# A transformer layer on eight cores: the output projection of two heads spread over the two heads behind them, with more buffers and the transposes in another PSUM pair

## Chip, cores and metric

The kernel runs on one Trainium2 chip, on all 8 cores. Each core works on one sequence of 2048 tokens, with no exchange between cores. The metric is the device time in microseconds of the slowest core; a change of under 2% counts as none.

## What is computed

One layer with pre-normalisation, per sequence of shape 2048 x 1024, 8 heads of 256, a latent of 64 for keys and values, and a gated feed-forward part of width 3072 with integer weights:

```python
q = (x @ Wq.T).reshape(b, t, N_HEADS, HEAD_DIM)
kv_latent = x @ Wkv_down.T                    # 64 wide
k = (kv_latent @ Wk_up.T).reshape(...)
v = (kv_latent @ Wv_up.T).reshape(...)
attn = softmax(einsum('bqhd,bkhd->bhqk', q, k) * HEAD_DIM ** (-0.5))
out = einsum('bhqk,bkhd->bqhd', attn, v)
x = x + out.reshape(b, t, -1) @ Wo.T          # all on layernorm(x)
h = silu(xn @ wg.T) * (xn @ wu.T)             # xn = layernorm(x), w = int / 127
x = x + h @ wd.T
```

## The kernel before

**Work of a head.** The kernel never forms k, v or the full q. As the latent has only 64 values, it folds Wk_up into Wq and Wv_up into Wo for each head, and attention runs in the latent space. All activations are held with features on partitions. Names used below, with the lines of the kernel before:

- `emit_prepA`, `emit_prepB` (L283, L303): the folded query weight, 64 x 1024, and its transpose, which goes into the buffer WAT. PE writes both into PSUM pair PD, VectorE copies them out (L299, L321).
- `emit_prepC` (L326): the folded output weight of the head, 64 x 1024, into one of the MSB buffers (L342).
- `emit_Qp(h, tb)` (L347): the latent query of 512 tokens, 8 matmuls of 128 rows into a bank of PB.
- `emit_Spair(h, j, kp)` (L411): the scores of query block j (512 tokens, j from 0 to 3) against two blocks of 128 keys: two matmuls of 64 rows into PA or PD in turn; ScalarE takes the exponential of both (L434).
- `emit_PVg(h, j, qs)` (L442): 16 matmuls of 65 columns for 128 queries, the last column being the sum of the exponentials, into bank qs % 2 of PC. VectorE evacuates it with three instructions: a copy of the sum (L452), a reciprocal (L454), a product (L457) into the buffer UTM.
- `emit_UT(h, oct)` (L461): 8 small matmuls that transpose 1024 tokens of that result; ScalarE copies them into a buffer UFM (L486).
- `emit_WO2(h1, o, oct)` (L491), called a unit here: the output projection of two heads, h1 - 1 and h1, for 128 features o and 1024 tokens. It is 4 matmuls of 64 rows, 2 for each bank of PB or PC (in turn from unit to unit), and one add of VectorE onto x (L507). A pair of heads has 16 units.

**PSUM.** There are four pairs of banks, PA to PD, 1024 columns of float32 each. `bank_free` holds for each bank the instruction that last emptied it, and `pe_group` makes the first matmul of a group wait for it. A unit has two groups, one for each bank, so it has two such waits.

**Order.** Every engine works in the order in which the builder emits. Waits are on counters of the engines. The order is written by hand: the loop of a head (L657) first has block 0 of the scores, then for j = 1, 2, 3 and i = 0 to 3, called slot (j, i), two score pairs of block j, a PV group of block j - 1, and then what `fill` holds for the slot. For the next head these are prepA in (1,1), prepB in (2,1), Qp in (2,3), (3,0), (3,2), (3,3), and prepC in (3,1). The even heads 2, 4 and 6 have in addition the 16 units of the pair before them, two in each of the slots (1,0) to (2,3), ahead of what else stands there. Heads 0, 1, 3, 5 and 7 have none. Behind the slots come the four PV groups of block 3, the first score pairs of the next head and the two transposes. At the end of an odd head, four more score pairs, (nxt, 1, 0) to (nxt, 1, 3), are computed ahead, so that slots (1,0) and (1,1) of heads 2, 4 and 6 have none left. Behind head 7 come its transposes and the 16 units of heads 6 and 7, then the second layer norm and the feed-forward part.

**Buffers.** `arena` is one tensor in SBUF with offsets set by hand. MSB has three buffers of 1024 columns, used by h % 3; UFM is one area of two buffers, used by h % 2.

Of the kernel before, what the change touches and what calls it, by code (L numbers as in the profile page):

```python
# [18 lines left out]
NCH = 8  # L19
# [24 lines left out]
QP = QH  # L44
KVT = KH
WAB = KH + 1040
WAT = (VH, VH + 512)
MSB = (VH + 1024, VH + 2048, VH + 3072)
UTM = ZT
UFM = ZF  # L50
HHB = RA
WDB = VH
WG = (WQ0, WQ0 + 1024)
# [57 lines left out]
def build_program(tap=None):  # L111
# [22 lines left out]
    ar = ar_t.ap()  # L134
# [7 lines left out]
    PA = nc.alloc_psum_tensor("PA", [128, 1024], F32).ap()  # L142
    PB = nc.alloc_psum_tensor("PB", [128, 1024], F32).ap()
# [115 lines left out]
    qpev = [[None] * NTB for _ in range(H)]  # L259
    prepA_ev = [None] * H  # L260
    wat_done = [None, None]
    msb_done = [None] * 3
    ut_done = [[None, None], [None, None]]
    q_mm_done = [0] * H
    wo_mm_done = [0] * H
    wo_add_last = [0] * NCH
# [59 lines left out]
    def emit_prepC(h):  # L326
        key = ("prepC", h)
        if key in emitted:
            return
        emitted.add(key)  # L330
        wob = wo_base[h % 2]
        g = None
        for half in (0, 1):
            g = pe_group(
                PD[0:64, half * 512:(half + 1) * 512], [("PD", half)],
                [(ar[:, WVU + (h * 2 + c) * 64: WVU + (h * 2 + c + 1) * 64],
                  ar[:, wob + c * 1024 + half * 512:
                     wob + c * 1024 + (half + 1) * 512])
                 for c in (0, 1)],
                waits=[(sWS, ws_all), (sWO[h % 2], 16 * (h // 2 + 1))])  # L340
# [120 lines left out]
    def emit_UT(h, oct_):  # L461
        key = ("UT", h, oct_)
        if key in emitted:
            return
        emitted.add(key)
        ti = s_rot[0] % 2
        s_rot[0] += 1
        P = (PA, PD)[ti]
        keys = [("PA", 0), ("PA", 1)] if ti == 0 else [("PD", 0), ("PD", 1)]
        w = [(sDVE, zev_done[(h, 2 * oct_ + 1, 3)]), (sPOOL, pool_init)]  # L470
        for k in keys:
            tf = bank_free.get(k)
            if tf:
                w.append(tf)
        for i in range(8):
            tc = oct_ * 8 + i
            b.emit("tensor", lambda e, tc=tc, i=i, P=P: e.matmul(
                P[0:64, i * 128:(i + 1) * 128],
                ar[:, UTM + tc * 64: UTM + (tc + 1) * 64],
                ident, start=True, stop=True),  # L480
                waits=w if i == 0 else (),
                inc=sPE if i == 7 else None)
        g = sPE.n
        ub = UFM + (h % 2) * 2048
        dst = ar[0:64, ub + oct_ * 1024: ub + (oct_ + 1) * 1024]
        v = consume("scalar", lambda e, P=P, d=dst: e.activation(  # L486
            d, P[0:64, 0:1024], AF.Copy),
            keys, waits=[(sPE, g)], inc=sACT)
        ut_done[h % 2][oct_] = (sACT, v)

    def emit_WO2(h1, o, oct_):  # L491
        P, pk = ((PB, "PB"), (PC, "PC"))[wo_pair[0] % 2]
        wo_pair[0] += 1
        h0 = h1 - 1
        g = None
        for n in (0, 1):
            tb = oct_ * 2 + n
            g = pe_group(
                bank(P, n), [(pk, n)],
                [(ar[0:64, MSB[hh % 3] + o * 128: MSB[hh % 3] + (o + 1) * 128],  # L500
                  ar[0:64, UFM + (hh % 2) * 2048 + tb * 512:
                     UFM + (hh % 2) * 2048 + (tb + 1) * 512])
                 for hh in (h0, h1)],
                waits=[msb_done[h0 % 3], msb_done[h1 % 3],
                       ut_done[0][oct_], ut_done[1][oct_]])
        wo_add_last[o] = consume(
            "vector", lambda e, P=P, o=o, oc=oct_: e.tensor_add(  # L507
                x[:, o * T + oc * 1024: o * T + (oc + 1) * 1024], P[:, 0:1024],
                x[:, o * T + oc * 1024: o * T + (oc + 1) * 1024]),
            [(pk, 0), (pk, 1)], waits=[(sPE, g), (sX, 16)], inc=sDVE)  # L510
# [146 lines left out]
    for h in range(H):  # L657
# [15 lines left out]
        if nxt < H:  # L673
# [289 lines left out]
```

How the kernel before makes its waits and increments, by code:

```python
        def run(e, wl=wl, fn=fn, after=after):  # L100
            for (hh, v) in wl:
                e.wait_ge(hh, v)
            inst = fn(e)
            if after is not None:
                inst.then_inc(after[0], after[1])
# [5 lines left out]
def build_program(tap=None):  # L111
# [764 lines left out]
                b.emit("sync", lambda e, o=o: e.dma_start(  # L876
                    out=out_d[o * 128:(o + 1) * 128, :],
                    in_=x[:, o * T:(o + 1) * T]),
                    waits=[(sDVE, down_add_final)], inc=sST)
        down_b1_done[0] = sPE.n
        if half == 0:
            for c in range(NHALF, NFC):
                load_wd(c, [(sPE, down_b1_done[0])] if c == NHALF else [])
    fin = sST.n
    b.emit("sync", lambda e: e.wait_ge(sST.h, fin))
    with nc.Block() as block:
        @block.tensor
```

## Time and profile before

| | us |
|---|---|
| median of 2 runs | 1258.91 (1257.81 and 1260.01) |
| the profiled execution | 1260.86 |
| its span on core 4, the slowest (the cores: 1249.8 to 1259.0) | 1259.0 |
| PE busy with matmuls | 1116.6 (89%) |
| VectorE busy | 358.0 (28%) |
| ScalarE busy | 417.1 (33%) |
| GpSimd busy | 55.1 (4%) |

The span is the time from the first to the last instruction of a core. All rows and times below are of core 4, in us from the start of its span. The profile's page has a line with the clock that TensorE was granted in each fortieth of the span, in tenths of 2.4 GHz. There are two levels, 1.2 GHz (0.50) and 2.4 GHz (1.00); numbers in between are means over a stretch. Attention fills the time up to about 695 us, the rest is the second layer norm and the feed-forward part.

### The profile page before, as it was taken

The numbers are of one execution on the slowest core, as the hardware profiler recorded it, in microseconds if no ns is written. First come the engines' busy times: TensorE is split into PE (matmuls) and PEld (weight loads), VectorE is DVE, ScalarE is ACT, GpSimd is POOL, SyncE is SP. The second block draws the span as 40 slices with busy tenths as digits, with TensorE's granted clock in tenths as the row PEclk, the third lists the DMA queues.
The fourth block names the chain that finished last, engine by engine and source line by source line (L and its number), as shares of the span: only waits on it lengthen the run. The fifth ranks groups of instructions, "written<-read, shape, count | busy, mean of one in ns | idle before, by whom it ended". The sixth has DMA issues, their size and how long they took to land.

```text
span 1259.0 us, 15601 instructions; the slowest of 8 cores (1249.8 to 1259.0 us)
## 1 busy us (share of the span) xinstructions
PE 1116.6 (89%) x5873; PEld 477.0 (38%) x5921; DVE 358.0 (28%) x674; ACT 417.1 (33%) x402; POOL 55.1 (4%) x110
## 2 busy tenths in 40 slices
PE   7656989898898998889899577999999999999998
PEld 3112433333343343433343122444444444444443
DVE  0573222243223441334226452010112201010122
ACT  0313565523644346532674122233200022233000
POOL 2000000000000000000001200000000020000000
PEclk9876576756666575855856677999999999999999
DMA  8941101010110010000005902222210082221122
GB/s 131 250 124 17 18 17 18 17 18 7 28 18 1 17 18 1 1 1 1 1 1 101 163 4 33 35 34 42 42 17 1 1 135 34 42 42 18 67 101 100
DMA packets 17561, 54.08 MB, mean 43 GB/s; under 512 B 1744, under 2 KB 1872, under 8 KB 15440
## 3 DMA queue, kind: packets, MB, share of 16 engines
q0 software_dynamic: 15296, 36.31, 18.1%
q1 hardware_dynamic: 2192, 16.78, 3.6%
q8 instruction: 48, 0.79, 0.3%
q14 instruction: 25, 0.20, 0.1%
HBM read 72.61 MB, written 8.39 MB: 64 GB/s over the span
## 4 chain that ended last, share of the span: by engine, by line
PE 76%; ACT 10%; DVE 7%; DMA 3%; issue 3%; DVEq 0%; ACTq 0%; POOL 0%; POOLq 0%
PE PB L179 23%; PE PA L179 19%; PE PC L179 18%; PE PD L179 15%; ACT arena L434 7%; DMA arena<-x 2%; DVE arena L624 1%; DVE arena L622 1%; DVE x_fm L507 1%; ACT arena L486 1%; DVE arena L342 1%; DVE arena L299 1%; ACT arena L527 1%; DVE arena L321 0%; DMA arena<-x_fm 0%
## 5 line engine op out<-in xcount | busy, mean ns | idle before, releaser
L179 PE MATMUL PA<-arena 128*128 128x512 bf16 (+2 forms) x1066 | 301.4, 424 | 30.6 <-DMA arena<-x 9.2
L179 PE MATMUL PB<-arena 128*128 128x512 bf16 (+2 forms) x1129 | 305.7, 422 | 3.3 <-DVE arena L321 1.3
L179 PE MATMUL PC<-arena 128*128 128x65 bf16 (+3 forms) x2584 | 277.9, 272 | 23.2 <-DVE arena L624 16.6
L179 PE MATMUL PD<-arena 128*128 128x512 bf16 (+3 forms) x774 | 249.0, 452 | 39.6 <-ACT arena L434 22.7
L179 PEld LDWEIGHTS PC<-arena 128*128 128x128 bf16 (+2 forms) x2592 | 158.6, 117 | 196.0 <-issue 151.1
L434 ACT ACTIVATE arena<-PA 128x1024 bf16<-128x1024 f32 x121 | 123.8, 1023 | 272.8 <-PE PA L179 258.2
L179 PEld LDWEIGHTS PB<-arena 128*128 128x128 bf16 (+2 forms) x1152 | 118.9, 108 | 152.1 <-issue 43.3
L179 PEld LDWEIGHTS PA<-arena 128*128 128x128 bf16 (+2 forms) x1074 | 99.1, 101 | 180.7 <-issue 84.6
L434 ACT ACTIVATE arena<-PD 128x1024 bf16<-128x1024 f32 x135 | 138.1, 1023 | 28.7 <-PE PD L179 18.0
L179 PEld LDWEIGHTS PD<-arena 128*128 128x128 bf16 (+3 forms) x782 | 77.1, 106 | 177.1 <-issue 120.3
L826 DVE TENSOR_TENSOR arena<-arena 128x1024 bf16<-128x1024 bf16 x48 | 33.2, 692 | 302.1 <-ACT arena L817 302.1
L452 DVE COPY t<-PC 128x1 f32<-128x1 f32 x128 | 20.2, 158 | 243.1 <-PE PC L179 241.1
L812 ACT ACTIVATE arena<-PA 128x1024 bf16<-128x1024 f32 x24 | 24.6, 1023 | 137.6 <-PE PA L179 137.6
L507 DVE TENSOR_TENSOR x_fm<-PB,x_fm 128x1024 f32<-128x1024 f32 x32 | 39.2, 1224 | 29.2 <-PE PB L179 29.1
L812 ACT ACTIVATE arena<-PC 128x1024 bf16<-128x1024 f32 x24 | 24.6, 1023 | 57.5 <-PE PC L179 57.4
L507 DVE TENSOR_TENSOR x_fm<-PC,x_fm 128x1024 f32<-128x1024 f32 x32 | 39.2, 1225 | 15.0 <-PE PC L179 13.9
L817 ACT ACTIVATE arena<-PD 128x1024 bf16<-128x1024 f32 x24 | 24.6, 1023 | 56.7 <-PE PD L179 56.7
L817 ACT ACTIVATE arena<-PB 128x1024 bf16<-128x1024 f32 x24 | 24.6, 1023 | 54.6 <-PE PB L179 54.6
L457 DVE TENSOR_SCALAR arena<-PC,rc 128x64 bf16<-128x64 f32 x128 | 36.3, 284 | 13.7
L871 DVE TENSOR_TENSOR x_fm<-PB,x_fm 128x1024 f32<-128x1024 f32 x16 | 19.6, 1224 | 63.3 <-PE PB L179 63.3
L871 DVE TENSOR_TENSOR x_fm<-PA,x_fm 128x1024 f32<-128x1024 f32 x16 | 19.6, 1224 | 62.0 <-PE PA L179 62.0
L362 DVE CAST arena<-PB 64x512 bf16<-64x512 f32 x32 | 21.8, 683 | 49.1 <-PE PB L179 49.1
(71 smaller groups left out, 311.9 us busy)
## 6 DMA issues: line engine op xcount, KB each, us to landing
x_fm<-x SPq DMA_DIRECT2D x1, 8192.0 KB, 43.1
out<-x_fm SPq DMA_DIRECT2D x8, 1024.0 KB, 3.8
arena<-wg POOLq DMA_DIRECT2D x24, 256.0 KB, 3.9
arena<-wu POOLq DMA_DIRECT2D x24, 256.0 KB, 3.6
arena<-wd POOLq DMA_DIRECT2D x24, 256.0 KB, 15.0
arena<-x POOLq DMA_DIRECT2D x1, 4096.0 KB, 30.4
arena<-wq POOLq DMA_DIRECT2D x8, 512.0 KB, 5.7
arena<-wo POOLq DMA_DIRECT2D x8, 512.0 KB, 5.5
```

Source lines behind the costliest of these rows:

```text
L179: e.matmul(o, l, r, start=st, stop=sp)),
L299: prepA_ev[h] = consume("vector", lambda e: e.tensor_copy(ar[0:64, WAB:WAB + 1024], PD[0:64, 0:1024]), [("PD", 0), ("PD", 1)], waits=[(sPE ...
L342: v = consume("vector", lambda e, h=h: e.tensor_copy(ar[0:64, MSB[h % 3]:MSB[h % 3] + 1024], PD[0:64, 0:1024]), [("PD", 0), ("PD", 1)], wa ...
L362: v = consume("vector", lambda e, a=qa, d=dst: e.tensor_copy(d, a[0:64, :]), [qk], waits=[(sPE, g)], inc=sDVE)
L434: "scalar", lambda e, P=P, p=pbuf, kp=kp: e.activation(ar[:, p + kp * 1024: p + (kp + 1) * 1024], P[:, 0:1024], AF.Exp, scale=SC_ATTN),
L452: b.emit("vector", lambda e, a=za: e.tensor_copy(t1[:, 0:1], a[:, 64:65]), waits=[(sPE, g)], inc=sDVE)
L457: "vector", lambda e, a=za, tc=tc: e.tensor_scalar_mul(ar[:, UTM + tc * 64: UTM + (tc + 1) * 64], a[:, 0:64], rc),
L507: "vector", lambda e, P=P, o=o, oc=oct_: e.tensor_add(x[:, o * T + oc * 1024: o * T + (oc + 1) * 1024], P[:, 0:1024], x[:, o * T + oc * 10 ...
L812: "scalar", lambda e, t=t: e.activation(ar[:, SCR_S:SCR_S + 1024], G_ap[t][:, 0:1024], AF.Silu, scale=INV127),
L817: "scalar", lambda e, t=t: e.activation(ar[:, SCR_U:SCR_U + 1024], U_ap[t][:, 0:1024], AF.Copy, scale=INV127 * INV127),
L826: "vector", lambda e, hcol=hcol: e.tensor_mul(ar[:, hcol:hcol + 1024], ar[:, SCR_S:SCR_S + 1024], ar[:, SCR_U:SCR_U + 1024]),
L871: "vector", lambda e, P=P, o=o, tp=tp: e.tensor_add(x[:, o * T + tp * 1024: o * T + (tp + 1) * 1024], P[:, 0:1024], x[:, o * T + tp * 1024 ...
```

## The change

It has three parts.

1. Units of a pair of heads are spread over two heads. The first eight (o from 0 to 3) stay in the even head behind the pair, the other eight (o from 4 to 7) move to the odd head after it. Each of the slots (1,0) to (2,3) of heads 2 to 7 now has one unit. The 16 units behind head 7 stay.
2. For that, buffers must live longer: MSB has four buffers (h % 4), UFM three (h % 3). WAT moves to free columns in the key area, and MSB takes the place that it had.
3. The transposes of `emit_UT` go to PB, both of them. Before, they took PA or PD in turn with the score pairs.

```diff
-WAT = (VH, VH + 512)
-MSB = (VH + 1024, VH + 2048, VH + 3072)
+WAT = (KH + 2064, KH + 2576)
+MSB = (VH, VH + 1024, VH + 2048, VH + 3072)
 UTM = ZT
-UFM = ZF
+UFM = (ZF, ZF + 2048, ZT + 1024)
...
-    msb_done = [None] * 3
-    ut_done = [[None, None], [None, None]]
+    msb_done = [None] * 4
+    ut_done = [[None, None] for _ in range(3)]
...
     def emit_UT(h, oct_):
...
-        ti = s_rot[0] % 2
-        s_rot[0] += 1
-        P = (PA, PD)[ti]
-        keys = [("PA", 0), ("PA", 1)] if ti == 0 else [("PD", 0), ("PD", 1)]
+        P = PB
+        keys = [("PB", 0), ("PB", 1)]
...
-        ub = UFM + (h % 2) * 2048
+        ub = UFM[h % 3]
...
     def emit_WO2(h1, o, oct_):
...
-                waits=[msb_done[h0 % 3], msb_done[h1 % 3],
-                       ut_done[0][oct_], ut_done[1][oct_]])
+                waits=[msb_done[h0 % 4], msb_done[h1 % 4],
+                       ut_done[h0 % 3][oct_], ut_done[h1 % 3][oct_]])
...
+        wu = []
         if h % 2 == 0 and h > 0:
-            wu = [(o, oc) for o in range(NCH) for oc in (0, 1)]
-            for idx, (o, oc) in enumerate(wu):
-                slot = (1 + idx // 8, (idx % 8) // 2)
-                fill.setdefault(slot, []).insert(0, (lambda o=o, oc=oc:
-                                                     emit_WO2(h - 1, o, oc)))
+            wu = [(h - 1, o, oc) for o in range(4) for oc in (0, 1)]
+        elif h % 2 == 1 and h >= 3:
+            wu = [(h - 2, o, oc) for o in range(4, NCH) for oc in (0, 1)]
+        for idx, (h1, o, oc) in enumerate(wu):
+            slot = (1 + idx // 4, idx % 4)
+            fill.setdefault(slot, []).insert(0, (lambda h1=h1, o=o, oc=oc:
+                                                 emit_WO2(h1, o, oc)))
```

How PE's order moves, at three places. All rows are PE's, in the order of the program, with the counter that a matmul waits for, if any (sACT is ScalarE's, sDVE VectorE's). 128x65 is a PV group, 128x512 into PA or PD a score pair, 128x512 into PB or PC a unit, 64x512 into PD prepA, 64x128 a transpose.

Head 2, slots (1,0) and (1,1) with prepA behind them, before:

```order
L179 MATMUL PC<-arena 128x65 x16
L179 MATMUL PB<-arena 128x512 x4
L179 MATMUL PC<-arena 128x512 [waits sDVE]
L179 MATMUL PC<-arena 128x512 x3
L179 MATMUL PC<-arena 128x65 [waits sDVE]
L179 MATMUL PC<-arena 128x65 x15
L179 MATMUL PB<-arena 128x512 x4
L179 MATMUL PC<-arena 128x512 x2
L179 MATMUL PC<-arena 128x512 [waits sDVE]
L179 MATMUL PC<-arena 128x512
L179 MATMUL PD<-arena 64x512 [waits sWQ1,sACT]
```

The same place after the change:

```order
L179 MATMUL PC<-arena 128x65 x16
L179 MATMUL PB<-arena 128x512 x4
L179 MATMUL PC<-arena 128x65 x16
L179 MATMUL PC<-arena 128x512 [waits sDVE]
L179 MATMUL PC<-arena 128x512
L179 MATMUL PC<-arena 128x512 [waits sDVE]
L179 MATMUL PC<-arena 128x512
L179 MATMUL PD<-arena 64x512 [waits sWQ1,sACT]
```

The second PV group no longer waits for VectorE, and the unit in PC stands directly behind it, with a wait ahead of each half.

Head 3, slot (1,1) with prepA behind it, before:

```order
L179 MATMUL PA<-arena 128x512 [waits sACT]
L179 MATMUL PA<-arena 128x512
L179 MATMUL PD<-arena 128x512 [waits sACT]
L179 MATMUL PD<-arena 128x512
L179 MATMUL PC<-arena 128x65 x16
L179 MATMUL PD<-arena 64x512 [waits sWQ0,sACT]
```

The same place after the change:

```order
L179 MATMUL PA<-arena 128x512 [waits sACT]
L179 MATMUL PA<-arena 128x512
L179 MATMUL PD<-arena 128x512 [waits sACT]
L179 MATMUL PD<-arena 128x512
L179 MATMUL PC<-arena 128x65 x16
L179 MATMUL PC<-arena 128x512 [waits sDVE]
L179 MATMUL PC<-arena 128x512
L179 MATMUL PC<-arena 128x512 [waits sDVE]
L179 MATMUL PC<-arena 128x512
L179 MATMUL PD<-arena 64x512 [waits sWQ0,sACT]
```

A unit in PC stands between the PV group and prepA. Slots with an even i have their unit in PB.

Behind head 7, the transposes and the first units, before:

```order
L477 MATMUL PA<-arena 64x128 x8
L477 MATMUL PD<-arena 64x128 [waits sDVE]
L477 MATMUL PD<-arena 64x128 x7
L179 MATMUL PB<-arena 128x512 [waits sACT]
L179 MATMUL PB<-arena 128x512 x3
```

The same place after the change:

```order
L475 MATMUL PB<-arena 64x128 x8
L475 MATMUL PB<-arena 64x128 [waits sDVE,sACT]
L475 MATMUL PB<-arena 64x128 x7
L179 MATMUL PB<-arena 128x512 [waits sACT]
L179 MATMUL PB<-arena 128x512 x3
```

The second transpose waits for ScalarE too, and both it and the first unit use the pair that the first transpose used.

## Rows read from the trace of the kernel before

**Rows 1.** The page: granted TensorE clock in 40 slices, in tenths.

```profile
PEclk9876576756666575855856677999999999999999
```

**Rows 2.** Stretches of heads 3 and 6: busy us of each engine, then the clock.

```profile
324.20:384.60 60.40, 53.93 (x385) 23.40 (x386) 15.77 (x56) 34.85 (x35) 1.06 (x2) 0.66 0.10 18
531.10:619.50 88.40, 79.65 (x449) 32.00 (x450) 35.11 (x71) 34.80 (x35) 0.00 (x0) 0.63 0.00 1
```

**Rows 3.** Stretches within heads 1 and 2, columns PE, PEld, DVE, ACT, POOL, clock, DMA.

```profile
211.10:221.30 10.20, 7.89 (x60) 3.44 (x58) 3.79 (x9) 4.87 (x5) 0.53 (x1) 1.00 0.00 0
...
262.00:283.00 21.00, 21.00 (x91) 8.33 (x90) 10.27 (x19) 6.14 (x6) 0.00 (x0) 0.50 0.04 7
...
298.00:306.70 8.70, 8.70 (x35) 3.63 (x35) 2.51 (x5) 2.05 (x2) 0.00 (x0) 0.50 0.01 3
306.70:327.20 20.50, 16.78 (x174) 8.37 (x171) 7.50 (x25) 12.01 (x12) 0.53 (x1) 1.00 0.16 27
```

**Rows 4.** Order of time, PE, head 3: start, us, instruction, idle before and releaser.

```profile
337.66 1.89 PE L179 MATMUL PD<-arena 128*64 128x512 bf16 x4 [0.58 <-ACT arena L434]
...
345.83 1.03 PE L179 MATMUL PA<-arena 64*128 64x512 bf16 x2
...
348.64 1.03 PE L179 MATMUL PA<-arena 64*128 64x512 bf16 x2
...
352.11 0.58 PE L314 MATMUL PD<-arena 64*128 64x64 bf16 x8 [0.59 <-ACT arena L434]
...
353.70 1.01 PE L179 MATMUL PD<-arena 64*128 64x512 bf16 x2 [0.16 <-DVE arena L321]
```

**Rows 5.** Order of time, PE, head 2, slots (1,0) and (1,1).

```profile
245.35 1.06 PE L179 MATMUL PC<-arena 128*128 128x65 bf16 x16
246.34 1.88 PE L179 MATMUL PB<-arena 64*128 64x512 bf16 x4
248.02 1.91 PE L179 MATMUL PC<-arena 64*128 64x512 bf16 x4
251.48 1.04 PE L179 MATMUL PC<-arena 128*128 128x65 bf16 x16 [1.55 <-DVE x_fm L507]
```

**Rows 6.** Order of time, VectorE, the same place.

```profile
246.58 0.16 DVE L452 COPY t<-PC 128x1 f32<-128x1 f32 x1 [12.14 <-PE PC L179]
...
247.11 0.28 DVE L457 TENSOR_SCALAR arena<-PC,rc 128x64 bf16<-128x64 f32 x1
248.47 1.22 DVE L507 TENSOR_TENSOR x_fm<-PB,x_fm 128x1024 f32<-128x1024 f32 x1 [1.07 <-PE PB L179]
```

**Rows 7.** Order of time, PE, single places in heads 1, 2 and 7.

```profile
209.92 2.49 PE L179 MATMUL PB<-arena 128*64 128x512 bf16 x8
...
236.41 0.61 PE L477 MATMUL PA<-arena 128*64 128x128 bf16 x8 [0.52 <-ACT arena L486]
...
286.33 1.01 PE L179 MATMUL PD<-arena 64*128 64x512 bf16 x2 [1.06 <-DVE arena L321]
...
298.01 3.62 PE L179 MATMUL PB<-arena 128*64 128x512 bf16 x8
...
661.05 1.92 PE L179 MATMUL PC<-arena 128*128 128x65 bf16 x32 [0.70 <-DVE rc L454]
663.23 1.96 PE L179 MATMUL PC<-arena 128*128 128x65 bf16 x32 [0.26 <-DVE arena L457]
```

**Rows 8.** Order of time, ScalarE and PE, the transposes and first units behind head 7.

```profile
665.90 1.02 ACT L486 ACTIVATE arena<-PA 64x1024 bf16<-64x1024 f32 x1 [5.11 <-PE PA L477]
666.32 0.61 PE L477 MATMUL PD<-arena 128*64 128x128 bf16 x8 [0.57 <-DVE arena L457]
667.06 1.02 PE L179 MATMUL PB<-arena 64*128 64x512 bf16 x4
667.08 1.02 ACT L486 ACTIVATE arena<-PD 64x1024 bf16<-64x1024 f32 x1 [0.16 <-PE PD L477]
668.24 1.02 PE L179 MATMUL PC<-arena 64*128 64x512 bf16 x4 [0.16 <-ACT arena L486]
```

More of the change, by code:

```diff
@@ L342, in emit_prepC @@
         v = consume("vector", lambda e, h=h: e.tensor_copy(
-            ar[0:64, MSB[h % 3]:MSB[h % 3] + 1024], PD[0:64, 0:1024]),
+            ar[0:64, MSB[h % 4]:MSB[h % 4] + 1024], PD[0:64, 0:1024]),
             [("PD", 0), ("PD", 1)], waits=[(sPE, g)], inc=sDVE)
-        msb_done[h % 3] = (sDVE, v)
+        msb_done[h % 4] = (sDVE, v)
     def emit_Qp(h, tb, eng="vector"):
@@ L488, in emit_UT @@
             keys, waits=[(sPE, g)], inc=sACT)
-        ut_done[h % 2][oct_] = (sACT, v)
+        ut_done[h % 3][oct_] = (sACT, v)
     def emit_WO2(h1, o, oct_):
@@ L499, in emit_WO2 @@
                 bank(P, n), [(pk, n)],
-                [(ar[0:64, MSB[hh % 3] + o * 128: MSB[hh % 3] + (o + 1) * 128],
-                  ar[0:64, UFM + (hh % 2) * 2048 + tb * 512:
-                     UFM + (hh % 2) * 2048 + (tb + 1) * 512])
+                [(ar[0:64, MSB[hh % 4] + o * 128: MSB[hh % 4] + (o + 1) * 128],
+                  ar[0:64, UFM[hh % 3] + tb * 512:
+                     UFM[hh % 3] + (tb + 1) * 512])
                  for hh in (h0, h1)],
-                waits=[msb_done[h0 % 3], msb_done[h1 % 3],
-                       ut_done[0][oct_], ut_done[1][oct_]])
+                waits=[msb_done[h0 % 4], msb_done[h1 % 4],
+                       ut_done[h0 % 3][oct_], ut_done[h1 % 3][oct_]])
         wo_add_last[o] = consume(
@@ L740, in build_program @@
             maybe_tap("u0", ar[:, UTM:UTM + 1024], [(sDVE, zev_done[(0, 3, 3)])])
-            maybe_tap("uf0", ar[0:64, UFM:UFM + 2048], [ut_done[0][1]])
+            maybe_tap("uf0", ar[0:64, UFM[0]:UFM[0] + 2048], [ut_done[0][1]])
     pe_attn_done = sPE.n
```

## Prediction

> **What bounds the kernel now.** I read the page first, then stretches by head, then the order of time on TensorE (PE). The page's line of the granted clock has 5 to 8 tenths in slices 2 to 25 of 40, which hold all of attention, and 9 after them [rows 1]. The stretches by head say the same: head 3, which today has no output-projection units, takes 60.4 us at a mean clock of 0.66; head 6, which has sixteen, 88.4 us at 0.63; ScalarE is busy some 34.8 us in either, so it is not what bounds a whole head [rows 2]. Each head has two phases. In its slots (1,0) to (2,3) the clock stands at 1.2 GHz (0.50); from the query projection Qp of the next head to the head's end it is mostly at 2.4 GHz [rows 3]. All units of emit_WO2, before and after the change, lie in the slow phase of their heads, apart from the sixteen behind head 7.
>
> In that phase PE has no slack. In head 3 one slot (two score pairs and a PV group) goes from 345.83 to 348.64, 2.81 us [rows 4]. A unit costs PE 248.02 - 246.34 = 1.68 us on top [rows 5]. From 262 to 283 us, where each slot of head 2 has two units, PE is busy 21.00 of 21.00 us at 0.50 [rows 3].
>
> **Eight units moved per pair of heads.** Eight units leave heads 2, 4 and 6 (8 x 1.68 = 13.4 us each) and eight enter heads 3, 5 and 7 (13.4 us each). No work is removed, both places run on a PE-bound stretch at the same clock, so the sum is nil: 3 x (13.4 - 13.4) = 0. ScalarE gains nothing either: a slot with one unit is 2.81 + 1.68 = 4.5 us of PE against two exponentials, each of about the 1.02 us that ScalarE's copies of the same width take [rows 8]. What is left is waits.
>
> A page of the Trainium skill speaks for more. "TensorE: Matmul & The Clock Gate", Part 1, says that the clock goes by how busy PE has been and that sustained activity brings full rate. By that, filling the idle time of the light heads would lift them to 2.4 GHz. The trace disagrees: the stretch from 262 to 283 us is full and stays at 0.50 [rows 3]. By the rule the sum would be that of rival C; by the rows it is nil.
>
> **Waits that go.** (a) Slot (1,1) of heads 2, 4 and 6 has its score pairs computed ahead, so the PV group stands directly behind a unit in PC and waits 1.55 us for VectorE's add [rows 5]. After the change one unit in PB stands ahead of it, and that wait goes: -1.55 x 3. (b) In heads 3 and 5 prepA waits 0.58 us and prepB 0.59 us for the exponential in PD [rows 4]. The PC unit now ahead of each hides that: -1.17 x 2.
>
> **Waits that come.** (c) With one unit per slot, PB and PC take turns by slot, so slots with odd i have PV in bank 1 of PC and, directly behind it, the unit in PC. Its second half needs bank 1, which is free when VectorE has evacuated the PV group. In head 2 a PV group starts at 245.35 [rows 5]; its evacuation starts with the copy at 246.58 and ends at 247.11 + 0.28 = 247.39 [rows 6], 2.04 us after the start of PV. With 0.14 us from an end to the next start (668.10 to 668.24 [rows 8]) the bank is free at 2.18. PE gets there after the PV group (246.34 - 245.35 = 0.99 us) and half a unit (0.84), at 1.83. So it waits 0.35 us. Today the PB unit in between covers this. There are four such slots in each of six heads, 24, less the three of (d): 21 x 0.35 = +7.4. Queued behind the waiting matmul are the rest of the unit and, in order, everything else of PE; nothing else can fill the time.
> (d) In slot (1,1) of heads 2, 4, 6 VectorE first adds the PB unit: from 248.47 for 1.22 us, to 249.69 [rows 6]. PV starts at 248.02 already, its evacuation (0.81 us from the copy's start to its end) only after 249.69, so it ends at 250.50 and the bank is free at 250.64. PE arrives at 248.02 + 0.99 + 0.84 = 249.85: +0.79 x 3.
> (e) prepB in heads 3 and 5: the second score pair behind it waits for the copy of L321, 0.16 us today [rows 4]. With a unit's add ahead of that copy on VectorE it will wait as in head 2, 1.06 us [rows 7]: +0.90 x 2.
> (f) The transposes of head 7: both now use PB. The second starts at 666.32 today [rows 8]; it must then wait for ScalarE's copy of the first (665.90 + 1.02 + 0.14 = 667.06), +0.74. Its own copy starts 0.76 us after it (667.08 - 666.32), takes 1.02, and the first output unit, in PB too, starts 0.14 later: 667.06 + 0.76 + 1.02 + 0.14 = 668.98 against 667.06 today: +1.92. The units behind it go at the pace of VectorE or PE as before.
> (g) In heads 0 to 6 the transposes lose nothing: the second waits for ScalarE's copy of the first today too (0.52 us at 236.41 [rows 7]), through PA. The score pairs between them no longer share a bank with them, but ScalarE is then working back to back. I count nil, at best 0.2 us per head.
> The moved buffers cost nothing: no instruction is added, and no load waits for them before the end of attention. A wait on a third buffer of transposed values or a fourth of MSB comes a head later than its last reader.
>
> Sum: -4.65 - 2.34 + 7.35 + 2.37 + 1.80 + 1.92 = +6.5 us. The only term without a direct row is (c). Other waits of PE for the evacuation of a PV group are 0.70 and 0.26 us [rows 7]; below, it cannot be under 0, since a bank is either free or waited for. With 0 the sum is -0.9, with 0.70 it is +13.8. I take 0.35, which is worked out of starts and ends of the same three instructions and lies next to the 0.26. The profiled execution took 1260.86 us (span 1259.0); 1260.86 + 6.5 = 1267.4. The median of the plain runs, 1258.91, is 1.95 us below the profiled one, so I predict 1265.4 us, 0.5% over it.
>
> **Rivals.** A is the forecast.
> B: the waits of (c) are hidden, PE reaching bank 1 when it is free. For it: the margin is a third of a microsecond, and PE idles elsewhere in some slots. Against: (c) comes from unhurried rows. 1258.9 - 0.9 = 1258.0 us.
> C: light heads filled with units come up to 2.4 GHz. A slot of 4.5 us would take half, 2.25 (ScalarE's two exponentials just fit): 2.25 x 8 slots x 3 heads = 54 us, 1265.4 - 54 = 1211 us. Against: both a stretch with no units (light slots) and one with two per slot stay at 0.50, and one unit per slot lies between them. Only the rule of the Trainium skill quoted above speaks for it.
> D: the clock comes up later in heads 3 and 5. In head 1, without units, it is up from 211.1; Qp(nxt,0) had begun at 209.92. In head 2, with units just ahead of Qp, it comes up only at 306.7, and Qp had begun at 298.01: 0.50 from 298 to 306.7 [rows 3, 7]. If the unit ahead of Qp does this, heads 3 and 5 lose up to 8 us each of full clock, worth up to half, some 3.5 us each: 1265.4 + 7 = 1272.4.
> E, the other side: D in its strong form. The unit and its wait directly ahead of Qp keep the clock at 1.2 GHz for the whole 20.5 us that head 2 now has at 2.4 GHz [rows 3]. PE is busy 16.78 us of these [rows 3], which is up to 33.6 at half rate, 13 us more than the stretch takes now. Two heads of it already decide (25 us is 2%): 1265.4 + 26 = 1291. Against: the sixteen-unit heads have two units directly ahead of Qp and come up all the same.
>
> **How the numbers follow.** A 0.53, B 0.15, C 0.04, D 0.24, E 0.04. A's own range is 1261 to 1270; the cores of this run differ by 9 us in when their clock falls and rises, and each head can shift by a few. B adds 1258 below, D 1274 above: 1257 to 1274, with C and E left out. A change of under 2% is about what a measurement of this kernel cannot tell from none; faster by over 2% is C (0.04), slower by over 2% is E (0.04), the rest 0.92.
>
> **What would show it.** In the new trace: PC matmuls waiting for the last step of a PV evacuation 24 times, 0.35 us each and 0.8 in three; the 1.55 us waits for the add gone; heads 2 to 6 all 72 to 77 us; the light heads' slots at 0.50 and 4.5 us; the first unit behind head 7 some 1.9 us after the second transpose, 0.7 today. If slots of head 3 run at 2.4 GHz, or the waits of (c) are absent, or Qp(nxt,0) of head 3 begins over 5 us before the clock comes up, the forecast is wrong at that step.

## The result, and the profile after

| | median us | ratio to the kernel before, 95% interval |
|---|---|---|
| kernel before, beside it | 1260.31 | |
| changed kernel | 1265.86 | 1.0052 [1.0038, 1.0065] |

The change costs half a per cent, 5.6 us; 0.5% was forecast, 6.5 us, and 1265.4 us. That 1265.4 and 1265.86 lie so close is in part luck: the forecast started from 1258.91 us for the kernel before, which measures 1260.31 here, and its difference was 1 us too large.

The slowest core is now core 6, and the rows after the change are of that core. Its span went from 1258.9 us to 1264.5; averaged over the eight cores the span went from 1255.1 to 1262.4 us, since the cores lay further apart before. The page's line of the granted clock answers to [rows 1]:

```profile
PEclk9777586758576575857655777999999999999999
```

It still has 5 to 8 tenths all through attention. The six heads that now hold eight units each, as stretches with the busy time of PE, PEld, VectorE, ScalarE and GpSimd, then the clock; they answer to [rows 2]:

```profile
231.80:306.30 74.50, 65.84 (x417) 26.12 (x416) 25.31 (x63) 34.73 (x35) 1.06 (x2) 0.66 0.09 15
306.30:381.40 75.10, 67.55 (x418) 27.10 (x417) 25.38 (x64) 34.60 (x35) 1.06 (x2) 0.64 0.09 15
381.40:457.80 76.40, 67.58 (x417) 26.80 (x416) 25.32 (x64) 34.97 (x35) 1.06 (x2) 0.64 0.09 14
457.80:533.00 75.20, 67.71 (x418) 27.23 (x417) 25.34 (x64) 34.78 (x35) 0.00 (x0) 0.64 0.00 1
533.00:607.10 74.10, 66.06 (x418) 26.20 (x417) 25.34 (x64) 34.77 (x35) 0.00 (x0) 0.65 0.00 1
607.10:668.30 61.20, 55.93 (x362) 24.64 (x361) 19.16 (x55) 31.79 (x32) 0.00 (x0) 0.53 0.00 1
```

Heads 2 to 6 now have one length, 74.1 to 76.4 us, where they had 58 to 60 and 88 to 90 in turn. That is what the spreading does: it moved time and saved none.

The new waits stand in PE's order of time, in head 2: start, duration, instruction, idle before it and its releaser. They answer to [rows 5].

```profile
244.22 1.89 PE L179 MATMUL PB<-arena 64*128 64x512 bf16 x4
246.04 2.03 PE L179 MATMUL PC<-arena 128*128 128x65 bf16 x18
248.64 1.01 PE L179 MATMUL PC<-arena 64*128 64x512 bf16 x2 [0.57 <-DVE arena L457]
...
258.49 2.03 PE L179 MATMUL PC<-arena 128*128 128x65 bf16 x18
260.69 1.01 PE L179 MATMUL PC<-arena 64*128 64x512 bf16 x2 [0.17 <-DVE arena L457]
```

"x18" is the PV group (16) with the first half of the unit (2), since both write PC. In the second case, slot (1,3), it starts at 258.49, and the second half follows at 260.69: 2.20 us, where the prediction had 2.18. Without a wait PE would have been there after 1.83, so the wait costs 0.37 us. The bracket says only 0.17, as the end of a matmul is modelled in the profile and here lies some 0.2 us behind the point at which the next may start. Whoever adds up brackets would count half of this wait. In slot (1,1) of head 2 it is 248.64 - 246.04 = 2.60, so 0.77 us (0.79 forecast).

The waits of PE in total, from 160 to 700 us (engine, line, releaser: us in total, times, longest):

```profile
PE PB L475 <- ACT arena L484: 10.8, 8, 1.5
...
PE PC L179 <- DVE arena L457: 5.8, 25, 0.6
PE PD L179 <- DVE arena L321: 5.5, 6, 1.1
...
PE PB L179 <- ACT arena L484: 1.3, 1, 1.3
```

25 waits for L457: the 24 forecast and the one that was already there at the end of head 7 [rows 7]. None for the add of a unit is left; that was the 1.55 us wait of [rows 5]. The place behind head 7, which answers to [rows 8]:

```profile
668.27 1.06 PE L475 MATMUL PB<-arena 128*64 128x128 bf16 x8
...
670.65 0.61 PE L475 MATMUL PB<-arena 128*64 128x128 bf16 x8 [1.31 <-ACT arena L484]
...
672.57 1.74 PE L179 MATMUL PB<-arena 64*128 64x512 bf16 x4 [1.31 <-ACT arena L484]
```

From the second transpose to the first unit it is 1.92 us, as forecast.

Where did the 5.6 us of this core come from? The starts of the first transpose of each head, read from the order of time of core 6, give the account. I name an interval by the head whose slots it holds, and give before, after and what is left when the 13.4 us of moved units are taken out:

| interval | before | after | left | forecast |
|---|---|---|---|---|
| up to the first transpose of head 0 | 173.83 | 173.63 | -0.2 | 0 |
| head 1 | 60.12 | 58.16 | -2.0 | 0 |
| head 2 | 90.08 | 74.55 | -2.1 | +0.3 |
| head 3 | 60.34 | 75.05 | +1.3 | +1.1 |
| head 4 | 88.11 | 76.42 | +1.7 | +0.3 |
| head 5 | 58.40 | 75.19 | +3.4 | +1.1 |
| head 6 | 88.38 | 74.10 | -0.9 | +0.3 |
| head 7 | 45.64 | 61.17 | +2.1 | +1.4 |
| from the transposes of head 7 to the end | 594.0 | 596.2 | +2.2 | +1.9 |

Heads 2 to 7 have +5.5 together and +4.5 was forecast. On core 0 they have 436.5 us against 428.9, +7.5. Single heads are off by up to 2.4 us to either side. Head 1 is off by 2.0 us, though its slots are unchanged: its mean granted clock on core 6 was 0.66 before and is 0.71 now, while core 0 has 0.71 and 58.15 us in both kernels. So part of the differences of single heads is the clock, to which the experiments come.

### The profile page after: what moved, and what is told of

Same layout as the page of the kernel before. It is cut to its first block, busy times and chain, and to the rows that moved or that the text cites. A ratio compares the mean times of both kernels' runs of the same rounds, so it can differ in the third digit from the quotient of the medians.

```text
span 1264.5 us, 15636 instructions; the slowest of 8 cores (1260.0 to 1264.5 us)
## 1 busy us (share of the span) xinstructions
PE 1120.6 (89%) x5921; PEld 471.6 (37%) x5921; DVE 358.1 (28%) x674; ACT 417.0 (33%) x402; POOL 55.1 (4%) x110
## 4 chain that ended last, share of the span: by engine, by line
PE 74%; ACT 9%; DVE 9%; issue 3%; DMA 3%; DVEq 0%; ACTq 0%; POOL 0%; POOLq 0%
PE PB L179 24%; PE PA L179 19%; PE PC L179 17%; PE PD L179 15%; ACT arena L434 6%; DMA arena<-x 3%; ACT arena L484 1%; DVE arena L620 1%; DVE arena L622 1%; DVE x_fm L505 1%; DVE arena L299 1%; DVE arena L342 1%; ACT arena L525 1%; DVE arena L457 1%; DVE arena L321 0%
## 5 line engine op out<-in xcount | busy, mean ns | idle before, releaser
L179 PE MATMUL PA<-arena 128*128 128x512 bf16 (+2 forms) x1088 | 306.6, 423 | 24.1 <-DMA arena<-x 10.2
L179 PE MATMUL PC<-arena 128*128 128x65 bf16 (+3 forms) x2592 | 281.1, 272 | 23.1 <-DVE arena L622 16.6
L179 PE MATMUL PD<-arena 128*128 128x512 bf16 (+3 forms) x768 | 242.6, 449 | 42.2 <-ACT arena L434 24.8
L179 PEld LDWEIGHTS PC<-arena 128*128 128x128 bf16 (+2 forms) x2592 | 150.1, 115 | 193.6 <-issue 147.3
L434 ACT ACTIVATE arena<-PA 128x1024 bf16<-128x1024 f32 x128 | 130.9, 1023 | 273.3 <-PE PA L179 260.3
L179 PEld LDWEIGHTS PA<-arena 128*128 128x128 bf16 (+2 forms) x1088 | 103.0, 102 | 184.8 <-issue 89.3
L434 ACT ACTIVATE arena<-PD 128x1024 bf16<-128x1024 f32 x128 | 131.0, 1023 | 29.8 <-PE PD L179 20.9
L813 ACT ACTIVATE arena<-PA 128x1024 bf16<-128x1024 f32 x24 | 24.6, 1023 | 137.6 <-PE PA L179 137.6
L818 ACT ACTIVATE arena<-PD 128x1024 bf16<-128x1024 f32 x24 | 24.6, 1023 | 55.6 <-PE PD L179 55.6
L457 DVE TENSOR_SCALAR arena<-PC,rc 128x64 bf16<-128x64 f32 x128 | 36.3, 284 | 14.2 <-DVE rc L454 0.8
```

The lines of the kernel that those rows point to most:

```text
L179: e.matmul(o, l, r, start=st, stop=sp)),
L434: "scalar", lambda e, P=P, p=pbuf, kp=kp: e.activation(ar[:, p + kp * 1024: p + (kp + 1) * 1024], P[:, 0:1024], AF.Exp, scale=SC_ATTN),
L457: "vector", lambda e, a=za, tc=tc: e.tensor_scalar_mul(ar[:, UTM + tc * 64: UTM + (tc + 1) * 64], a[:, 0:64], rc),
L813: "scalar", lambda e, t=t: e.activation(ar[:, SCR_S:SCR_S + 1024], G_ap[t][:, 0:1024], AF.Silu, scale=INV127),
L818: "scalar", lambda e, t=t: e.activation(ar[:, SCR_U:SCR_U + 1024], U_ap[t][:, 0:1024], AF.Copy, scale=INV127 * INV127),
```

## The experiments

Each ran beside the kernel before on the same chip; the ratio is always to that kernel.

**1. Units in PB.** The waits for bank 1 of PC are taken away by giving the units of the slots to PB, except in slot (2,3), where Qp follows in PB.

```diff
-    def emit_WO2(h1, o, oct_):
-        P, pk = ((PB, "PB"), (PC, "PC"))[wo_pair[0] % 2]
-        wo_pair[0] += 1
+    def emit_WO2(h1, o, oct_, pair=None):
+        if pair is None:
+            pair = wo_pair[0] % 2
+            wo_pair[0] += 1
+        P, pk = ((PB, "PB"), (PC, "PC"))[pair]
...
-            fill.setdefault(slot, []).insert(0, (lambda h1=h1, o=o, oc=oc:
-                                                 emit_WO2(h1, o, oc)))
+            fill.setdefault(slot, []).insert(0, (lambda h1=h1, o=o, oc=oc, pair=int(idx == 7):
+                                                 emit_WO2(h1, o, oc, pair)))
```

> The changed kernel, with the units of the slots in PB, all but the one of slot (2,3), which stays in PC. Theory (the waits for bank 1 of PC cost what they take, 0.37 us from start to start): they go in 15 places (three slots each in six heads, less slot (1,1) of heads 2, 4 and 6, where the unit now waits about as long, 0.8 us, for the add of the unit ahead in PB), 15 x 0.37 = 5.5 us. The ratio to the kernel before falls from 1.005 to about 1.001. In the trace PE waits for L457 six or seven times outside head 7's end instead of 25. Rival (the time of the new kernel goes by when the clock comes up, and a few tenths of a microsecond of waits disappear in it): within 1.5 us of the changed kernel, ratio 1.004 to 1.006, although the waits are gone.

Measured: 0.9996 [0.9982, 1.0009]. Against the changed kernel's 1.0052 that is 0.56%, or 7 us; 5.5 were expected. The waits in the trace (core 0), 160 to 700 us:

```profile
PE PB L179 <- DVE x_fm L507: 1.7, 3, 0.6
...
PE PC L179 <- DVE arena L457: 1.3, 7, 0.3
```

Seven waits for L457 instead of 25, and three for the add, in slot (1,1) of heads 2, 4 and 6, as expected. So the units in PC are what makes the changed kernel slower: with them in PB the whole slowdown is gone. The waits themselves are 5.5 us of it. Heads 2 to 7 are 8.7 to 14.1 us shorter than in the changed kernel, core by core, so the edit also changed something beside the waits; run 5 comes back to it.

**2. Transposes back in PA and PD.**

```diff
-        P = PB
-        keys = [("PB", 0), ("PB", 1)]
+        ti = s_rot[0] % 2
+        s_rot[0] += 1
+        P = (PA, PD)[ti]
+        keys = [("PA", 0), ("PA", 1)] if ti == 0 else [("PD", 0), ("PD", 1)]
```

> The changed kernel, with the transposes back in PA and PD in turn with the score pairs. Theory (the new place of the transposes costs only behind head 7, where the second waits for the copy of the first, and the first unit for the copy of the second): 2.4 us less than the changed kernel, ratio 1.003; from the first transpose of head 7 to the first unit about 1.9 us instead of 4.3. Rival (it costs nothing, since the units behind it catch up, or it gains in the other heads): no change from 1.005, or above.

Measured: 1.0038 [1.0022, 1.0054], 0.14% or 1.8 us below the changed kernel. The difference is no larger than the two intervals allow, so the time alone shows little. The rows behind head 7 (core 4) do:

```profile
666.63 1.06 PE L477 MATMUL PA<-arena 128*64 128x128 bf16 x8
667.84 0.61 PE L477 MATMUL PD<-arena 128*64 128x128 bf16 x8
669.00 1.02 PE L179 MATMUL PB<-arena 64*128 64x512 bf16 x4 [0.56 <-ACT arena L486]
```

2.37 us from the first transpose to the first unit instead of 4.30: 1.93, where the forecast for this term was 1.92. The expected 1.9 us for this stretch was off, since the clock had not yet come up there (the first transpose takes 1.06 us, against some 0.6 at 2.4 GHz; in the kernel before the clock comes up with it).

**3. Both edits.** The spreading and its buffers are left, with seven of a head's eight units in PB.

> Both edits: units of the slots in PB but for slot (2,3), and the transposes in PA and PD as before. Only the spreading of the units is left of the change. Theory: the two savings add up, 5.5 + 2.4 = 7.9 us below the changed kernel, ratio about 0.999, which says that the spreading alone is neutral. Rival (spreading alone costs, by later rises of the clock in heads 3 to 5): ratio 1.002 or more.

Measured: 0.9962 [0.9945, 0.9979]. It is faster than the kernel before, by 0.2 to 0.55%, where 0.999 was expected. So the spreading itself does not cost; with its units in PB it gains a little. By the prediction's terms 4.65 + 2.34 us of waits go, 2.37 + 1.80 come, and six waits of 0.37 us are left in slot (2,3): -0.6 us. Measured are 2.7 to 6.9 us. The rest was not isolated. The moment at which the clock comes up moves by more than that from run to run (below), so I leave it open.

**4. Transposes alone.** The kernel before, with `P = PB` and its keys in `emit_UT`.

> The kernel before, with the transposes in PB and nothing else changed. Theory: only the place behind head 7 pays, 1.9 to 2.4 us, ratio 1.0015 to 1.002. The heads before it keep their lengths (58.4 and 88.1 us from transpose to transpose). Rival (free of the score pairs' banks the transposes shorten each head's end): ratio under 1.000 by up to 1 us per head.

Measured: 1.0018 [1.0003, 1.0033]. On core 0 the heads have 58.2, 88.3, 58.3, 88.3, 58.4 and 89.9 us from transpose to transpose, where before had 58.2, 88.3, 58.5, 88.1, 58.4 and 89.9. Behind head 7 (core 5):

```profile
665.38 0.63 PE L475 MATMUL PB<-arena 128*64 128x128 bf16 x8
667.33 0.61 PE L475 MATMUL PB<-arena 128*64 128x128 bf16 x8 [1.31 <-ACT arena L484]
669.25 1.86 PE L179 MATMUL PB<-arena 64*128 64x512 bf16 x4 [1.31 <-ACT arena L484]
```

The second transpose now waits 1.31 us and stands 1.95 us behind the first; from it to the first unit it is 1.92 us, where [rows 8] have 0.74. From the first transpose it is 669.25 - 665.38 = 3.87 us, where the kernel before has 1.94 (its first transpose starts at 665.12 and its first unit at 667.06 [rows 8]): 1.93 more. Done alone, the part costs what the prediction says it costs, and only there.

**5. Qp ahead of the unit.** In slot (2,3) of heads 2 to 6 the unit moves behind the first Qp of the next head.

```diff
+            at = 1 if slot == (2, 3) and nxt < H else 0
-            fill.setdefault(slot, []).insert(0, (lambda h1=h1, o=o, oc=oc:
+            fill.setdefault(slot, []).insert(at, (lambda h1=h1, o=o, oc=oc:
```

> The changed kernel, with the unit of slot (2,3) behind the first Qp of the next head instead of ahead of it (heads 2 to 6). Theory (a unit directly ahead of Qp delays the rise of the clock, which is rival D of the prediction): the clock comes up within about 4 us of Qp's start in heads 4 and 5 too, where it takes 8.8 us now, and the run gains 1.9 us of waits (5 x 0.37) and some 2 us more from the clock: ratio 1.001 to 1.003. Rival (it is chance where the rise falls): the delays of the five heads stay spread between 3 and 9 us, and only the 1.9 us are gained: ratio 1.003 to 1.004.

Measured: 1.0027 [1.0011, 1.0042]. For each head I read when Qp starts and when the clock comes up next. In the changed kernel it takes 5.0, 3.2, 8.9, 8.8 and 4.3 us in heads 2 to 6 (core 6, and the same on the others). Here it is 1.3, 1.8, 4.3, 1.9 and 4.5 on cores 0, 5 and 6, and at most 4.5 on any core. Head 4 in both, the changed kernel first (order of time, then stretches with the clock):

```profile
431.71 3.62 PE L179 MATMUL PB<-arena 128*64 128x512 bf16 x8
435.26 1.03 PE L179 MATMUL PA<-arena 64*128 64x512 bf16 x2
...
438.07 3.16 PE L179 MATMUL PB<-arena 128*64 128x512 bf16 x8
```

```profile
431.70:440.60 8.90, 8.90 (x35) 3.61 (x35) 2.51 (x5) 2.05 (x2) 0.00 (x0) 0.50 0.00 0
440.60:461.00 20.40, 16.69 (x174) 8.47 (x173) 7.50 (x25) 12.00 (x12) 0.53 (x1) 1.00 0.16 27
```

Now with Qp first (core 4):

```profile
428.40:432.70 4.30, 4.30 (x13) 1.50 (x11) 1.07 (x4) 0.56 (x1) 0.00 (x0) 0.50 0.00 0
432.70:460.00 27.30, 22.64 (x205) 10.93 (x203) 9.56 (x30) 15.22 (x15) 0.53 (x1) 0.94 0.12 21
```

Half the time at 1.2 GHz after Qp's start, with PE full in both. The gain is only 0.25%, 3 us. Five of the waits for L457 go (19 left instead of 24), 1.9 us, but a new wait appears, longer in total, since the score pairs between the unit in PC and the next PV group are shorter at 2.4 GHz than VectorE's add:

```profile
PE PC L179 <- DVE x_fm L505: 3.4, 5, 0.7
```

So what this run gains is not waits; the clock comes up sooner. It does not follow that the instruction directly ahead of Qp decides it. Run 1 leaves the unit of slot (2,3) ahead of Qp, in PC and with its wait, and there the clock comes up in head 4 after 2.6 us (core 2), where it took 8.9:

```profile
425.69 1.01 PE L179 MATMUL PC<-arena 64*128 64x512 bf16 x2 [0.17 <-DVE arena L457]
426.63 3.20 PE L179 MATMUL PB<-arena 128*64 128x512 bf16 x8
...
426.60:429.30 2.70, 2.70 (x8) 1.15 (x8) 1.22 (x1) 0.00 (x0) 0.00 (x0) 0.50 0.00 0
429.30:445.00 15.70, 13.31 (x111) 6.19 (x109) 5.69 (x16) 8.19 (x8) 0.53 (x1) 1.00 0.21 35
```

The traces of all eight cores say the same. Here are the time from the transposes of head 1 to those of head 7, and the five delays from Qp to the clock added up:

| kernel | heads 2 to 7, us | delays of heads 2 to 6, us |
|---|---|---|
| before | 428.9 (five cores), 431.0 (three) | 27, 17 |
| changed | 436.5 (all) | 30 |
| run 1, units in PB | 427.7 (six), 426.5, 422.4 | 14, 21, 17 |
| run 2, transposes back | 436.3 (six), 433.2, 430.4 | 30, 28, 22 |
| run 5, Qp first | 426.8 (three), 429.5 (five) | 14, 13 to 17 |

The delays fall as much in run 1, where nothing was reordered at Qp, as here; in run 2 they differ from core to core within one program; and in the kernel before the three cores with the short delays are the longer ones. So the changed kernel does lose time with its clock, some 7 to 10 us against run 5, but which property of its schedule holds the clock down was not isolated.

**6. Score matmuls over 128 rows.** This asks why the clock is down at all. The upper 64 rows of both operands are zero, so nothing of the result changes and no matmul has more columns.

```diff
+    for lo, hi in ((QH + 512, QH + 4096), (KVA, KVA + 2048)):
+        b.emit("vector", lambda e, lo=lo, hi=hi: e.memset(
+            ar[64:128, lo:hi], 0.0), inc=sDVE)
...
-                [(ar[0:64, KVA + kc * 128: KVA + (kc + 1) * 128],
-                  ar[0:64, qpb + j * 512: qpb + (j + 1) * 512])],
+                [(ar[:, KVA + kc * 128: KVA + (kc + 1) * 128],
+                  ar[:, qpb + j * 512: qpb + (j + 1) * 512])],
```

> The changed kernel, with the score matmuls over 128 rows instead of 64: the upper 64 rows of both operands are set to zero once at the start, so the result is the same and each matmul takes as long at a given clock. Theory (the clock stays at 1.2 GHz in the slots because a 64-row matmul uses half of the rows, full as PE is): the slots run at 2.4 GHz in whole or in part, a slot without a unit takes about 2.2 us (two exponentials) instead of 2.81 and heads 1 to 7 get shorter by 10 to 30 us each: ratio 0.86 to 0.95. Rival (the clock goes by columns or by idle time alone): granted clock in the heads as now (0.55 to 0.7), ratio 1.004 to 1.007.

Measured: 0.9394 [0.9365, 0.9423], 76 us less. Two slots of head 1 (core 5), as a stretch:

```profile
180.70:185.10 4.40, 3.40 (x40) 1.77 (x40) 1.41 (x7) 4.05 (x4) 0.00 (x0) 1.00 0.41 82
```

2.2 us a slot instead of 2.81 [rows 4], the clock at 1.00, ScalarE busy 4.05 of 4.40. The same slots of head 1 in the kernel before:

```profile
196.00:203.30 7.30, 6.99 (x57) 3.46 (x56) 1.34 (x7) 5.67 (x6) 0.00 (x0) 0.50 0.01 2
```

PE is busy 3.40 of 4.40 us here, less than the 6.99 of 7.30 there and the 21.00 of 21.00 of [rows 3], both at 0.50. So PE's busy time alone does not tell the clock: with the same matmuls over twice the rows it is up, though PE has more idle time. Where the units still use 64 rows, in head 2 from 236 to 256 us, the clock is between, 0.83. The rule that the prediction took from the Trainium skill, "TensorE: Matmul & The Clock Gate", Part 1, speaks of busyness; in these rows busyness was not enough, and the rows that the matmuls use made the difference.

**7. Units over 128 rows too.** The same edit for the operands of a unit, shown against run 6. The upper rows of MSB and UFM are cleared too.

```diff
-    for lo, hi in ((QH + 512, QH + 4096), (KVA, KVA + 2048)):
+    for lo, hi in ((QH + 512, QH + 4096), (KVA, KVA + 2048), (VH, VH + 4096), (ZF, ZF + 4096),
+                   (ZT + 1024, ZT + 3072)):
...
-                [(ar[0:64, MSB[hh % 4] + o * 128: MSB[hh % 4] + (o + 1) * 128],
-                  ar[0:64, UFM[hh % 3] + tb * 512:
+                [(ar[:, MSB[hh % 4] + o * 128: MSB[hh % 4] + (o + 1) * 128],
+                  ar[:, UFM[hh % 3] + tb * 512:
```

> As e6_scores_128, and the matmuls of the units over 128 rows as well, the upper rows zero. Theory (rows in use): the clock is at 2.4 GHz in the slots with units too, and also behind head 7; ratio at least 0.01 below that of e6_scores_128. Rival (columns or idle time alone): no difference from the changed kernel.

Measured: 0.9121 [0.9093, 0.9149], 0.027 below run 6. Stretch of head 2 (core 2), with a unit in each slot:

```profile
232.00:250.00 18.00, 12.45 (x129) 6.64 (x131) 10.54 (x23) 10.29 (x11) 0.53 (x1) 1.00 0.18 30
```

Full clock, and PE busy only 12.45 of 18 us. It waits for the banks of PC, as the order of time there shows:

```profile
236.44 1.11 PE L179 MATMUL PC<-arena 128*128 128x65 bf16 x17
238.26 0.59 PE L179 MATMUL PC<-arena 128*128 128x512 bf16 x2 [0.71 <-DVE arena L461]
...
240.40 0.68 PE L179 MATMUL PC<-arena 128*128 128x65 bf16 x16 [0.68 <-DVE x_fm L509]
240.91 1.02 PE L179 MATMUL PB<-arena 128*128 128x512 bf16 x4
```

From the PV group to the second half of the unit it is 1.82 us. Without a wait it would be 0.51 (240.91 - 240.40) and half a unit, 0.43: the wait of 0.37 us has become one of 0.88.

**8. Runs 7 and 3 together.** The edits of runs 1, 2, 6 and 7 in one kernel.

> As e7_all_128, with the two edits of e3_both (units in PB but for slot (2,3), transposes in PA and PD). Theory: at 2.4 GHz PE reaches bank 1 of PC even earlier against VectorE, whose times do not change, so the waits taken out are longer than 0.37 us; but ScalarE now bounds more of a head, so part of it is hidden: ratio 0.002 to 0.01 below e7_all_128. Rival (all hidden under ScalarE): same as e7_all_128.

Measured: 0.8944 [0.8918, 0.897], 0.018 below run 7 where at most 0.010 was expected. Heads 2 and 3 (core 3) have one clock and 56.7 and 54.0 us, where the changed kernel has 74.5 and 75.1:

```profile
212.80:269.50 56.70, 43.55 (x420) 22.08 (x419) 25.36 (x64) 34.80 (x34) 1.06 (x2) 1.00 0.11 20
269.50:323.50 54.00, 43.17 (x419) 22.06 (x418) 25.34 (x63) 34.80 (x34) 1.06 (x2) 1.00 0.12 21
```

The two edits together gained 0.9% at 1.2 GHz (changed kernel to run 3) and 1.8% at 2.4 GHz: PE gets to the bank sooner, VectorE frees it no sooner.

**9. The kernel before with 128 rows.** The edits of runs 6 and 7, made to the kernel before. Sixteen units in every second head, at the same clock.

> The kernel before with the edit of e7_all_128 (score and unit matmuls over 128 rows, upper rows zero), so the units stand sixteen in each of heads 2, 4 and 6. Theory (spreading is neutral only while PE bounds both kinds of slot at 1.2 GHz; at 2.4 GHz a slot without units is bounded by ScalarE, so units placed there are nearly free): this kernel is slower than e8_all_128_both, which has the spread without its waits, by some 0.7 us in each of 24 slots, about 17 us: ratio 0.905 to 0.912. Rival (spreading is neutral at either clock): within 4 us of e8_all_128_both, ratio 0.891 to 0.898.

Measured: 0.9204 [0.9167, 0.9242]. Spreading with its waits taken out (run 8) is worth 0.026, 33 us, at 2.4 GHz, more than the 17 us expected, where it was worth at most 0.55% at 1.2. The change as it stands (run 7) gains 0.008 over this kernel, where it had lost 0.005. Head 2 with its sixteen units and head 3 with none (core 3):

```profile
215.00:286.00 71.00, 52.20 (x449) 24.83 (x448) 35.03 (x71) 34.59 (x35) 1.06 (x2) 0.98 0.09 16
286.00:336.00 50.00, 37.07 (x386) 19.18 (x384) 15.83 (x58) 35.20 (x35) 1.06 (x2) 1.00 0.12 22
```

121 us for two heads, against 110.7 in run 8. In head 3's slots ScalarE sets the pace, as in run 6, so time that PE has left there is lost; in head 2 PE waits for VectorE, for a unit's add or for a copy with such an add ahead of it. Behind the first units:

```profile
230.51 0.68 PE L179 MATMUL PC<-arena 128*128 128x65 bf16 x16 [1.65 <-DVE x_fm L510]
...
236.45 0.59 PE L179 MATMUL PD<-arena 128*128 128x512 bf16 x2 [2.02 <-DVE arena L302]
```

**10. Run 7 with the transposes back.** The edits of runs 2, 6 and 7.

> As e7_all_128, with only the transposes back in PA and PD; the units keep taking PB and PC in turn. Theory (the 21 us between e7_all_128 and e8_all_128_both come from the waits for bank 1 of PC, the transposes cost only behind head 7): 2 to 4 us below e7_all_128, ratio 0.909 to 0.911. Rival (at 2.4 GHz the place of the transposes costs in every head): 8 us or more below e7_all_128, ratio 0.906 or less.

Measured: 0.9044 [0.9015, 0.9073], 0.0077 or 9.7 us below run 7. The rival holds: at 2.4 GHz their place costs more than behind head 7. On core 0 the heads have 58.7, 56.2, 58.3, 56.4, 58.4 and 45.2 us, where run 7 has 60.4, 57.8, 58.3, 58.0, 60.4 and 45.8, so heads 2, 3, 5 and 6 gain 1.6 to 2.0 us each. Part of it is the clock: between the transposes of head 1 and head 7 core 0 is at 1.2 GHz for 22.5 us in run 7 and for 1.9 here, and takes 340.7 and 333.1 us. Two cores of run 7 that are there for only 6.8 us take 336.2. By them some 4.5 of the 7.6 us go with the clock, and about 3 are left for the waits. Why the clock falls more often in run 7 was not tried.

**11. Packed units.** As run 8, with the two heads of a pair in the lower and upper 64 rows, so that a unit is two matmuls without padding.

```diff
-                [(ar[:, MSB[hh % 4] + o * 128: MSB[hh % 4] + (o + 1) * 128],
-                  ar[:, UFM[hh % 3] + tb * 512:
-                     UFM[hh % 3] + (tb + 1) * 512])
-                 for hh in (h0, h1)],
+                [(ar[:, MSB[(h1 // 2) % 2] + o * 128: MSB[(h1 // 2) % 2] + (o + 1) * 128],
+                  ar[:, UFM[(h1 // 2) % 2] + tb * 512:
+                     UFM[(h1 // 2) % 2] + (tb + 1) * 512])],
```

> As e8_all_128_both, but the 128 rows of a unit hold both heads of the pair, one in the lower and one in the upper 64, so a unit is 2 matmuls instead of 4 and nothing of it is padding (two pair buffers for MSB and for the transposed values). Theory (in e8_all_128_both a slot with a unit is still bounded by PE, 1.4 + 0.85 us with its waits, just above ScalarE's 2.23): 0.43 us less of PE work in each of 48 slots, of which half or more shows, 8 to 20 us: ratio 0.879 to 0.888. Rival (the adds of VectorE and the exponentials set the pace already): ratio 0.891 to 0.897. Second rival (with less PE work the granted clock falls back to 1.2 GHz in some slots): ratio above 0.897.

Measured: 0.8900 [0.8873, 0.8927], 1120.64 us beside 1258.78. The interval touches that of run 8, so a gain over it is likely but not settled; between the two expected bands, it agrees with neither. Half the matmul work of the units is gone, yet heads 3 and 5 keep their 54.1 us (54.3 in head 5); heads 4 and 6 lose 1.1 us each. In slots of head 3, from 290 to 299 us on core 2, PE is busy 7.11 us, VectorE 7.11 and ScalarE 6.66, so no engine is full, and which hand-over between them sets the pace was not isolated. Behind head 7 the clock is lower, in part as the second rival has it, though the ratio is not (core 2):

```profile
531.00:562.00 31.00, 16.39 (x79) 4.19 (x80) 21.36 (x25) 17.32 (x10) 8.54 (x17) 0.64 0.72 137
```

Run 8 has 1.00 in the same stretch on core 3 and 0.89 on core 2. This is the fastest version of the study, 11% below both kernels.

## Why the prediction was right, point by point

- **Moved work is nil.** Right. Heads 2 to 6 take 74 to 76 us and the clock in their slots stayed at 0.50. Run 3 puts the spreading, with its units in PB, at 0.2 to 0.55% faster, so nothing was lost by it.
- **(a) and (b), waits that go.** Right in place. In the changed kernel PE has no wait for a unit's add and one for prepB instead of the three of the kernel before.
- **(c), 0.35 us in 21 places.** Right: 24 waits with those of (d), 0.37 us from start to start; run 1 took 15 of them away and gained 7 us where 5.5 were due. The rest came with the clock, which the sum does not hold.
- **(d), 0.79 us in slot (1,1).** Right, 0.77.
- **(e), prepB's copy.** Right: L321 has six waits of up to 1.1 us, 5.5 us in all, where it had 3.7 before: +1.8 as forecast.
- **(f), behind head 7.** Right, 1.93 us in run 2 and in run 4 against 1.92. In the changed kernel 4.30 us pass from the first transpose to the first unit instead of 1.94; the other 0.43 us are the first transpose, which runs at 1.2 GHz there.
- **(g), nothing in the other heads.** Right at this clock (run 4), wrong at 2.4 GHz (run 10).
- **Rival B** fell with the 24 waits. **Rival C**, by the busyness of PE, fell: the light heads stayed at 0.50. Run 6 shows why. **Rival E** fell: after Qp the clock is down for 8.9 us at most.
- **Rival D** had 0.24, as something in place of the forecast. It happened beside it: in head 5 the clock came up 8.8 us after Qp, where it took 1.2 before on core 6 and 4.4 on core 0; in head 3, the one that the prediction named as a sign, it came up after 3.2. Beside the terms of the forecast only 1.0 us (core 6) to 3.0 us (core 0) are left for it, less than its 7: between 170 and 670 us the mean clock is 0.65 before and 0.64 after on both cores. The forecast counts nothing for this. Its reason, the unit directly ahead of Qp, is not borne out: run 1 has the same unit there and the short delays.
- **The spread of the cores.** The prediction put the 9 us between their spans down to the clock of the heads. From head 1's transposes to head 7's they differ by only 2 us, 428.9 to 431.0; the rest lies ahead of head 1's end and behind head 7.

The sum was right to a tenth of a per cent, but not each head: single heads missed by up to 2.4 us with both signs, and that these misses nearly cancel is luck. So is it that the clock cost so little against the kernel before, as runs 1 and 5 show how much of it there was to win back. A sum of waits is a forecast of the mean; the clock adds a spread to it that no row of the waits holds.

## What to carry to other kernels

When work is moved between two stretches that one engine bounds at one clock, count only waits: which bank or buffer each moved piece shares with the instruction directly ahead of it, and how long the engine that frees it takes from the start of that instruction. Measure such a wait from start to start, since the idle time in the profile showed half of it here. Expect the clock to move with such a change too: its part here, 1 to 3 us, was in no row. And when TensorE is full but the granted clock is at 1.2 GHz, look at how many rows the matmuls use before rearranging anything: here operands padded with rows of zeros were worth 9%, and the rearrangement that had cost 0.5% then gained 0.8%, and 2.6% once its waits were taken out.

## What the runs showed that I had not expected

- Matmuls over 128 rows, half of them zero, brought the granted clock of attention from 0.5 to 1.00 (run 6, two slots; run 8, whole heads), with PE less busy than before. Padding scores and units took the changed kernel from 1.0052 to 0.9121 of the kernel before, 117 us.
- The same two edits gain 0.9% at 1.2 GHz (changed kernel to run 3) and 1.8% at 2.4 GHz (run 7 to run 8). For the units alone it is 0.6 to 0.8% (changed kernel to run 1, run 2 to run 3) and 1.0% (run 10 to run 8), which the intervals do not tell apart.
- With the same unit, bank and wait directly ahead of Qp, the clock came up 2.6 us after it in run 1 and 8.9 us after it in the changed kernel.
- Fewer matmuls for the same result went with a lower clock: in the packed version it is 0.64 behind head 7 (core 2), where the padded one has 0.89 (core 2) and 1.00 (core 3).
